# Layer 1 of a two-layer kernel: four buffers for the state-space decays, two in SBUF and two in PSUM

## The reference

```python
xn = _layernorm(x); x = x + _L0_attn_ref(xn, ...) + _L0_ffn_ref(xn, ...)   # gated retention; top-2 experts
xn = _layernorm(x); x = x + _L1_attn_ref(xn, ...) + _L1_ffn_ref(xn, ...)   # selective scan; routed attention
```

```python
dA = jnp.exp(d_t[..., None] * A)                                     # the decay
h = dA * h + d_t[..., None] * b_t[:, None, :] * u_t[..., None]       # the state
y = jnp.einsum('bds,bs->bd', h, c_t)                                 # sum over the 16 states
```

## Time and profile before

| | |
|---|---|
| median of three executions | 1772.57 us (1769.11 to 1778.48) |
| the profiled execution | 1774.8 us, its span 1773.1 us |
| TensorE clock granted, mean | 0.969 |
| PE busy | 1620.7 us (91%), 13450 matmuls |
| DVE busy | 1477.5 us (83%), 2750 instructions |
| POOL busy | 1367.5 us (77%), 1114 |
| ACT busy | 1349.2 us (76%), 3230 |
| DMA | 252.31 MB, mean 142 GB/s |

### The profile page before, as it was taken

The page is one execution under the profiler, slowest core; times in us unless marked ns, Lnnn a source line. Parts: engine busy times, 40 slices in busy tenths (PEclk is TensorE's granted clock), DMA queues, the critical chain, the costliest instruction groups (busy, mean ns, idle before and its releaser), DMA issues.

```text
span 1773.1 us, 43498 instructions
## 1 busy us (share of the span) xinstructions
PE 1620.7 (91%) x13450; PEld 987.0 (56%) x13450; DVE 1477.5 (83%) x2750; ACT 1349.2 (76%) x3230; POOL 1367.5 (77%) x1114
## 2 busy tenths in 40 slices
PE   6788999999885888799999999999999999999988
PEld 3455687677563453465465456456556455545545
DVE  5787854356786989899989999999999999998996
ACT  5377877576663868878978978887887897797774
POOL 2059548862671188998999899899899999899995
PEclk9799999999988899999999999999999999999999
DMA  9633446596565743274373464445535446445430
GB/s 326 187 99 121 129 136 205 149 215 193 130 133 161 195 135 115 90 179 109 117 189 101 140 170 123 123 139 126 165 104 146 117 130 177 105 126 161 108 96 25
DMA packets 169963, 252.31 MB, mean 142 GB/s; under 512 B 31144, under 2 KB 114280, under 8 KB 169736
## 3 DMA queue, kind: packets, MB, share of 16 engines
q1 hardware_dynamic: 157448, 232.74, 46.5%
q0 software_dynamic: 12288, 16.79, 4.6%
HBM read 170.44 MB, written 75.86 MB: 139 GB/s over the span
## 4 chain that ended last, share of the span: by engine, by line
PE 37%; DVE 10%; issue 8%; ACT 7%; POOL 5%; DMA 1%; SPq 0%; DVEq 0%; ACTq 0%; POOLq 0%
PE bank L2382 32%; POOL HB L2333 3%; PE bank L2482 3%; DVE bank L2905 3%; DVE HB L2905 2%; ACT bank L2695 2%; POOL HB L2339 2%; DVE SU L2877 2%; ACT PR L2733 1%; DVE HB L2910 1%; ACT PT L2617 1%; PE bank L2510 1%; PE bank L2392 1%; DVE nmax L2936 0%; ACT PR L2726 0%
## 5 line engine op out<-in xcount | busy, mean ns | idle before, releaser
L2333 POOL TENSOR_TENSOR HB<-DD,BC 128x512 f32<-128x512 f32 x512 | 640.9, 1280 | 102.5 <-DMA DD<-SU 48.5
L2695 ACT ACTIVATE bank<-DD,A 128x512 f32<-128x512 f32 x512 | 349.4, 694 | 113.7 <-DVE HB L2910 72.4
L2339 POOL TENSOR_TENSOR HB<-HB,BC 128x512 f32<-128x512 f32 x256 | 324.4, 1284 | 30.7 <-DVE HB L2905 30.1
L2905 DVE TENSOR_TENSOR_SCAN bank<-bank,HB 128x512 f32<-128x512 f32 x256 | 310.8, 1214 | 21.9 <-ACT bank L2695 18.6
L2905 DVE TENSOR_TENSOR_SCAN HB<-bank,HB 128x512 f32<-128x512 f32 x256 | 310.0, 1211 | 10.3 <-ACT bank L2695 7.3
L2910 DVE TENSOR_TENSOR HB<-bank,BC 128x512 f32<-128x512 f32 x256 | 175.4, 685 | 15.9 <-DVE bank L2905 0.9
L2382 PE MATMUL bank<-HB,fold 128*32 128x512 f32 x1024 | 138.3, 612 | 20.5 <-DVE HB L2910 10.8
L743 POOL DMA_INDIRECT X<-expert_out_scratch,slot x64 | 108.0, 1687 | 40.6 <-issue 15.7
L2482 PEld LDWEIGHTS bank<-ident,PR 128*128 128x128 f32 x768 | 86.9, 142 | 82.9 <-issue 45.0
L2482 PE MATMUL bank<-ident,PR 128*128 128x128 f32 x768 | 114.6, 281 | 18.2 <-ACT PR L2733 8.7
L718 POOL TENSOR_SCALAR XSC<-XR,mv,scaled 128x256 f32<-128x256 f32 x64 | 94.2, 1476 | 41.1 <-DVE scaled L1383 36.4
(11 more groups left out here) (287 smaller groups left out, 3568.1 us busy)
## 6 DMA issues: line engine op xcount, KB each, us to landing
DD<-dd_scratch SPq DMA_DIRECT2D x488, 128.0 KB, 3.2
ROW<-row_scratch SPq DMA_DIRECT2D x64, 256.0 KB
BC<-ssm_scratch SPq DMA_DIRECT2D x128, 128.0 KB, 4.0
US<-us_scratch SPq DMA_DIRECT2D x32, 512.0 KB, 4.8
dd_scratch<-SU SPq DMA_DIRECT2D x16, 1024.0 KB, 6.0
us_scratch<-SU SPq DMA_DIRECT2D x15, 1024.0 KB, 6.5
XL<-sorted_scratch SPq DMA_DIRECT2D x78, 128.0 KB
expert_out_scratch<-YS SPq DMA_DIRECT2D x78, 128.0 KB
```

What stands on the lines that cost most here:

```text
L2333: done(pool.tensor_tensor(HB[:, c % HR], du, bc, ALU.mult), "dbu")
L2339: done(pool.tensor_tensor(h, h, bc, ALU.mult), "cg")
L2695: done(act.activation(PD[n % 2][:], delta, ACT.Exp, scale=A[:, k:k + 1]), "dA")
L2905: done(dve.tensor_tensor_scan(h if n % 2 else dA, dA, h, 0.0, ALU.mult, ALU.add), "scan")
```

## The change

The decays of odd chunks go to a new SBUF tile PS of two halves, those of even chunks go to the two PSUM banks 0 and 1 in turn. The function `decays(n)` names the place. Each place is used again after four chunks and not after two, and `decay` waits for chunk n - 4. An even scan works in its PSUM bank as before; an odd scan now reads the decay and dbu both from SBUF and writes HB as before. To make room for PS (4 KB in each partition), es and rows are no tiles of their own any more but the two halves of SelT. The table of the order is the same.

```diff
--- before.py
+++ after.py
@@ -2039,7 +2039,7 @@
         YR, X = sb("YR", [NQT, D]), sb("X1", [NT, D])
         ahead, ties = sb("ahead", [NT, 3]), sb("ties", [NT])
         ssq, fx = sb("ssq1", [NT]), sb("fx", [NT])
-        es, rows, part = sb("es", [T]), sb("rows", [T]), sb("part", [2])
+        es, rows, part = SelT[:, 0], SelT[:, 1], sb("part", [2])
         first, kinv = sb("first", [1]), sb("kinv", [1])
         nmax, sums, rec = sb("nmax", [4, 4]), sb("sums", [TILES, AH]), sb("rec", [TILES, AH])
         RX = sb("RX", [AH, DH])
@@ -2050,7 +2050,7 @@
         over = {n: ctx.enter_context(nc.semaphore("b_" + n)) for n in
                 ["s_in", "small_in", "light_in", "heavy_in", "late_in", "key_out", "x_in", "xn_in", "key_in", "window_in", "pad_out", "out_dma", "u_dma", "gate_dma", "ssm_dma", "dt_in",
                  "del_dma", "du_dma", "us_in"] + [f"dd_in{i}" for i in range(DDS)] + [f"bc_in{i}" for i in range(4)]}
-        PD, PY = PB[0:2], PB[2]
+        PS, PY = sb("PS", [2, T]), PB[2]
 
         def after(eng, kind, b, *which):
 
@@ -2068,6 +2068,10 @@
 
         def chunk(c):
             return divmod(c, NCH)
+
+        def decays(n):
+
+            return PS[:, n // 2 % 2] if n % 2 else PB[n // 2 % 2][:]
 
         def pair(g):
             return slice(2 * g, 2 * g + 2)
@@ -2687,12 +2691,12 @@
 
                 def decay(b, n):
                     delta = dd_loaded(act, b, n)[:, 0]
-                    if b == 0 and n < 2:
+                    if b == 0 and n < 4:
                         after(act, "asc", 0, 0)
-                    if n >= 2 or b:
-                        after(act, "scan" if n % 2 else "mult", *chunk(NCH * b + n - 2))
+                    if n >= 4 or b:
+                        after(act, "scan" if n % 2 else "mult", *chunk(NCH * b + n - 4))
                     k = 4 * (4 * (n // 16) + n % 4) + n // 4 % 4
-                    done(act.activation(PD[n % 2][:], delta, ACT.Exp, scale=A[:, k:k + 1]), "dA")
+                    done(act.activation(decays(n), delta, ACT.Exp, scale=A[:, k:k + 1]), "dA")
 
                 def project(b, i):
                     kind, what, j = PROJECTIONS[i]
@@ -2901,13 +2905,13 @@
                 def scan(b, n):
                     after(dve, "dA", b, n)
                     after(dve, "dbu", b, n)
-                    dA, h = PD[n % 2][:], HB[:, (NCH * b + n) % HR]
+                    dA, h = decays(n), HB[:, (NCH * b + n) % HR]
                     done(dve.tensor_tensor_scan(h if n % 2 else dA, dA, h, 0.0, ALU.mult, ALU.add), "scan")
 
                 def times_c(b, n):
                     bc = bc_loaded(dve, b, n)[:, 1]
                     after(dve, "scan", b, n)
-                    done(dve.tensor_tensor(HB[:, (NCH * b + n) % HR], PD[n % 2][:], bc, ALU.mult), "mult")
+                    done(dve.tensor_tensor(HB[:, (NCH * b + n) % HR], decays(n), bc, ALU.mult), "mult")
 
                 def skip(b, k):
                     after(dve, "fold", b, *range(4 * k, 4 * k + 4))
```

## The result

The changed kernel takes 1944.14 us (median of four, 1940.07 to 1947.06) against 1774.44 us; the ratio is 1.0957, with a 95% interval of 1.092 to 1.0994. It is slower, as forecast, but by 170 us and not by 243. The forecast was 2016 us, its range 1890 to 2090.

A forecast was written before the change was run, and what follows sets the result against it. PE, DVE and POOL were taken as nearly full side by side in layer 1 (95%, 93%, 92%). Start 609.4 + POOL's work 1054.4 + lock 310 + idle 30 + end 13.5 = 2017 us of span; median 2016, range 1890 to 2090.

The forecast's parts named there:

- The mechanism: Layer 1: odd scans with both inputs in SBUF make POOL stand still, as L1416 does to L718 in layer 0.
- The forecast case: Layer 1: POOL loses about a scan's length per odd scan, 1.0 to 1.3 us; 1963 to 2040 us; 60%.
- rival (3): Most odd scans arrive late in a POOL product and cost 0.3 to 0.9 us each; up to 1963 us; 17%.
- the lock: POOL's loss to 256 odd scans in layer 1, 1.21 us each: 310 us (189 to 366).
- so nearly each scan meets a product. Worst: ... freezes it: Layer 1: POOL is busy 92%; a scan arriving in a product's first half freezes it, 1.43 us; 1.21 taken.
- my bounds: POOL's loss per odd scan in layer 1: 0.74 us at best, 1.43 at worst.
- the price of 1.43: Worst loss of POOL per odd scan: 1.21 us plus a surplus of 0.22 from L2339 beside L2967.
- DVE's loss: POOL holds DVE's odd scans by at most 0.36 us each, 92 us in all, still under POOL's new sum.
- Idle time that is left: POOL's idle time in layer 1's stage falls from 95.8 to 30 us; the 47.4 for folds nearly vanish.
- The gain: ACT's earlier decays save DVE's scans 0 to 26 us of waits, 15 taken, only while DVE or PE sets the pace.
- The signs: Profile after: L2333 and L2339 310 us longer, POOL's share 95% or more, PE's about 80%, HB waits over 100 us.
- The edits at nothing: ACT's decays to SBUF (-25 to +29 us), the odd scan's own length, shared SelT and SP's transfers cost nothing.

The follow-up runs named there:

- one_sbuf_input: Changed kernel with even chunks in PSUM bank 0 alone, odd scans reading their second input from unused PSUM bank 1; 0.9986 times the kernel before.
- two_sbuf_inputs: Changed kernel with all even chunks in PSUM bank 0 alone (wait for n-2), odd chunks as in the change, bank 1 free; 1.0947 times the kernel before.
- both_matched: Kernel before plus a 370-column POOL product ahead of each L2339 and a 602-column DVE memset ahead of each odd scan; ratio 1.0895.
- pool_matched: Kernel before plus only a 370-column POOL product ahead of each L2339, DVE as before; ratio 1.0744.
- sbuf_depth2: Kernel before with odd chunks' decays in one SBUF tile, even ones in PSUM bank 0, waits for chunk n-2 as before; ratio 1.094.
- pool_writes_only: Changed kernel with POOL's 768 products replaced by memsets of the same tiles; 1805.9 us where the kernel before had 1806.8 on that chip.

## Why the prediction was right, and where its sizes were off

**The mechanism was right.** The cost was seen in layer 0's L1416 and L718, in no engine's busy time. Two SBUF inputs against one is now shown by the pair one_sbuf_input and two_sbuf_inputs.

**The forecast case itself did not come.** I gave 60% to 1.0 to 1.3 us per odd scan and 1963 to 2040 us. The measured 0.80 and 1944 us lie in rival (3), 0.3 to 0.9 us and up to 1963, to which I gave 17%. The range held because it reached down to 1890. Some of the nearness is luck: two errors of opposite sign, 104 us too much for the lock and 33 too little for the idle time, partly cancelled.

**The step "so nearly each scan meets a product. Worst: ... freezes it" was mis-sized.** I took 1.21 us of POOL per odd scan, and (1573.4 - 1367.5) / 256 = 0.80 is what it paid: 206 us where I had 310. Of this the products L2337 and L2343 have 181 us, 0.71 per odd scan; the rest fell on POOL's other instructions. I read the earlier trace rows as the rule, in which the product that had begun was the one to wait, and chose a value near that end. In the changed kernel this is the exception. Of the 256 odd scans 227 start within one of the products, but only 17 within 0.1 us of its start, the case for which I had taken 1.21; in 166 of the 227 the product ended within 1.4 us and the scan was held over 0.19 us, until 1.14 us after the product's start (standard deviation 0.01). Thirteen of the products in flight took over 2 us; six of them had begun within 0.02 us of the scan, and of the other seven most had been held by an instruction before it. A product that is due during the scan then loses the scan's 1.21 us less the 0.14 us at the end of the product before, and less some of its own start: 0.91 at 877.07. In all, 207 of the 768 products took over 1.4 us, 0.89 over their norm in the mean. The 0.80 lies at the lower end of my bounds (0.74), which came from the earlier trace rows, and the rule that I quoted from the Trainium skill ("SBUF — State Buffer", section "Who interferes with whom"), that whoever issues first keeps the lock, was the better guide: it had excluded the freezing. It would still have given 1.21, as it says nothing of the ends of an instruction that overlap.

**My reading of the earlier trace rows missed a row.** When POOL's L718 of 131.16 started, DVE was already at L1472, a product of two SBUF tiles, two of which ran back to back until 131.70; the scan of 131.62 came right behind them. So this L718 was not the first, and it doesn't speak against the rule. The other frozen product, L2339 of 626.86, has no such forerunner: what DVE ran at its start reads one operand from a bank. But the same pair stands in the changed kernel, 0.37 us apart as before and after as much idle time, and there DVE's L2971 was the one to wait (1.99 us for 1.20) while the product took its 1.28. The row of the kernel before, then the two of the changed kernel:

```profile
130.95 0.75 DVE L1472 TENSOR_TENSOR O<-O,hr 128x256 f32<-128x256 f32 x2
...
626.59 1.28 POOL L2343 TENSOR_TENSOR HB<-HB,BC 128x512 f32<-128x512 f32 x1 [1.26 <-DVE HB L2909]
...
626.96 1.99 DVE L2971 TENSOR_TENSOR SU<-Sel,SU 128x1024 f32<-128x1024 f32 x1
```

So POOL's idle time ahead of the product doesn't decide who waits. What does in this pair stays open; the price of 1.43 rested on it alone.

**DVE's loss.** I gave at most 0.36 us a scan, 92 us, and called it hidden. It is 0.50 (438.3 - 310.0 = 128 us), as a scan that meets a product waits until 1.14 us after the product's start, and it isn't hidden altogether: both_matched against pool_matched puts it at 1.5%, some 27 us.

**Idle time that is left.** I put 30 us, it is 63.3 (1323.6 - 1260.3). In one sum: 608.3 + 1054.4 + 205.9 + 63.3 + 13.4 = 1945.3. The lock's term was 104 too high, the idle term 33 too low. The waits for folds fell from 47.4 to 26.7 us, those for scans only from 30.1 to 26.6.

**The gain.** DVE's waits for decays fell from 25.9 to 13.6 us and didn't matter, as I had written for a stage that POOL sets. one_sbuf_input adds that without the lock the deeper odd side is worth nothing measurable either (-0.1%, interval -0.4 to +0.1). That doesn't settle my 15 us: only 7.3 of the 25.9 us stood ahead of odd scans, and no run has the deeper even side without the lock.

**The signs.** POOL's means rose, but L2337 and L2343 together by 181 us, not 310, and that is 0.71 us per odd scan, hardly above the 0.7 below which I had named rival (3). The maxima reached 2.79 us, the odd scan's mean rose to 1.71, which I had named as the sign that POOL holds DVE and not the reverse. Each holds the other. POOL's share of the stage is 95.2%, PE's 86% (I had said 80): its work, 1088.9 us at a clock of 0.99, became 1133.5 at 0.95, in a shorter stage than forecast. DVE's waits for POOL's HB rose to 53.1 us, not over 100, perhaps because much of that wait has moved inside the scan, where it counts as busy. The edits at nothing stayed so: ACT's decays take 725 ns to SBUF and 697 to PSUM.

## What to carry to other kernels

Before an operand moves from PSUM to SBUF, count how many SBUF inputs the DVE instruction then has, and what POOL does beside it: with two, and a POOL that reads SBUF all the time, each instruction cost POOL 0.80 us and DVE 0.50 here, and no semaphore wait shows it, only longer instructions. Look for the same kind of instruction elsewhere in the trace; when a few rows show a stall from its two sides, look at what both engines ran just before, and take the price from the pattern that will repeat, back-to-back instructions. A buffer that removes an engine's waits is worth nothing if that engine isn't the bound: sbuf_depth2 and the changed kernel cost the same (1.094 and 1.0957), with 232.7 and 26.5 us of ACT's idle time ahead of its decays.

## What the runs showed of the hardware

- The scan held by a product starts to work 0.14 us before the product's end, at 1.14 of 1.28 us, with a spread of 0.01 us in 166 cases of the changed kernel. The start is reckoned from the scan's end less its usual 1.21 us.
- POOL's memset doesn't contend with such a scan: in pool_writes_only 166 of them lay beside an odd scan with two SBUF inputs and none took over 532 ns; the 90 scans that met one have a median of 1215 ns.
- Who waits isn't settled by the distance of two starts: with DVE's product 0.37 us behind POOL's, POOL's took 2.71 us and DVE's 1.20 in the kernel before, 1.28 and 1.99 in the changed one.
- The decay on ACT took 725 ns to SBUF and 697 ns to PSUM in the same kernel, from the same SBUF input.
